# Adding two chunks of squares on VectorE ahead of TensorE's sums over the partitions

## The chip, the cores and the metric

The kernel runs on one core of one Trainium2 chip. The metric is device time in microseconds (us) of one execution. Five engines work side by side, each through its own in-order queue, and wait for one another only by semaphores: TensorE (PE; its weight loads are listed apart, as PEld), VectorE (DVE), ScalarE (ACT), GpSimd (POOL) and SyncE (SP), which issues transfers.

## The reference, cut to what matters

Two layers, each a cross-attention block and a mixture-of-experts block. The change lies in the second layer's cross-attention, a recurrence of three iterations over 4 batches of 512 tokens (`slots`) with 256 features:

```python
def rmsnorm(x, w, eps=EPS):
    return x * jax.lax.rsqrt(jnp.mean(x * x, axis=-1, keepdims=True) + eps) * w
...
for _ in range(NUM_ITERS):                       # 3
    sn = rmsnorm(slots, slot_norm_w)
    q_proj = sn @ Wq.T
    scores = jnp.einsum('bkd,bmd->bkm', q_proj, k_proj) * SCALE
    attn = jax.nn.softmax(scores, axis=-2)
    attn = attn / (jnp.sum(attn, axis=-1, keepdims=True) + EPS)
    updates = jnp.einsum('bkm,bmd->bkd', attn, v_proj)
    slots = gru_cell(updates, slots, gru_wih, gru_whh, gru_bih, gru_bhh)
```

What matters here is `mean(x * x)` over the 256 features of each token.

## The kernel before, in words

The slots of a batch lie turned in SBUF: features on the 128 partitions, in two chunks (`C = 2`), and the 512 tokens along the free dimension, `HT[h]` with the shape 128 x 2 x 512. A batch has 512 tokens in `TT = 4` tiles of `P = 128`. Two batches are worked on in turn, `h` = 0 and 1. There are 12 turns of the recurrence (the text calls them turn 0 to turn 11; `q` in the code): turns 0 to 5 are the three iterations of batches 0 and 1, turns 6 to 11 those of batches 2 and 3. `it` is the iteration: 0 in turns 0, 1, 6 and 7.

The order of the work on each engine is written out by hand in `ORDER_C`, a string of stage names for each engine that `stages_c` reads once per turn `k`. A name with `-` in front belongs to the turn before, a name with `k:` in front is done in turn k alone (`!6,7:` in all but 6 and 7), and the digit at its end is then the batch. What the change touches, with the lines of the kernel:

- ACT `sq` (L1146; in iteration 0 inside `slotT`, L1134) squares `HT[h]` into `squares(h)`, 128 x 2 x 512, a view of the buffer `S1[h]`, and adds 1 to the semaphore `slot_sq`.
- ACT `hi` (L1176; L1132 in iteration 0) rounds the slots to a high part, and DVE `lo` (L1584; L1516 in iteration 0, inside `slotT`) computes the rest, `HTS[h][:, 1]`.
- PE `ss` (L1816 to L1828) waits for `slot_sq` and sums the squares over the partitions: for each of the 4 token tiles and each of the 2 chunks a matmul with the squares as weights and one column of ones as the moving operand, the 2 chunks of a tile accumulated in one column of PSUM. The trace has each of these 8 matmuls in float32 as two instructions, so a turn has 16 (and 16 weight loads).
- DVE `ve` (L1526) waits for these sums, scales them to a mean and adds epsilon. POOL `power` (L941) raises it to -1/2. PE `rsb` (L1834) spreads the four columns of roots over the partitions and turns them into a row with 4 products (8 instructions), ACT `rs` (L1149) moves it out.
- PE `scores` (L1836 to L1847) multiplies the keys with the slots; DVE `mulA`, `mulB` (L1534) scale the scores by that row of roots, and the softmax follows on DVE and ACT (L1538, L1153, L1543, L1138, L1547). PE `upd` (L1857) multiplies with the values, DVE `upd` (L1559) divides, PE `uT` (L1624) turns the result, and the gates of the recurrent cell follow on PE as `ha`, `ra`, `na`, `za`, `hb`, `rb`, `nb`, `zb` (products of three matmuls each, L205 to L207), mixed with the other batch's turn. DVE `ga` (L1568, L1571) and `zb` (L1577, L1579) are parts of the cell on VectorE.

In the order of PE a turn begins with `-ha ... -ra`, then `ss`, then `-na`, then `rsb` and `scores` (in turns 6 and 7 `ss` comes behind `-na`, and `-za` lies between `ss` and `rsb`; in turns 8 and 9 the router's `logits` lie ahead of `ss` and its `lt` ahead of `rsb`). In the order of DVE a turn has `... 6:slotT2 7:slotT3 lo ve ... -ga ...`; in turn 0 `0:slotT0 0:ctxT1` stand ahead of `lo ve`. `ctxT1` is L1511. PE `spin` (L1630) is a run of products of ones that nobody reads.

Around the recurrence: ahead of it the first layer (up to some 470 us of the span), behind it the second layer's routing and experts (from some 900 us).

Of the kernel before, what the change touches and what calls it, by code (L numbers as in the profile page):

```python
# [18 lines left out]
P = 128  # L19
# [10 lines left out]
C = D // P  # L30
# [69 lines left out]
def build(nc, x, ctx_in, cols, rows, wq, wk, wv, wo, pos_bias, w1, w2, router1, m1_w1, m1_w2, ws1, ws2,  # L100
          Wq, Wk, Wv, wih, whh, router2, gate_w, up_w, down_w, down_b, out):
    top = ExitStack()
    with top:
        def sb(name, shape, dt=F32, where=None):
            return (where or top).enter_context(nc.sbuf_tensor(name, shape, dt))
# [3 lines left out]
        def sem(name):  # L109
            if name not in sems:  # L110
                sems[name] = top.enter_context(nc.semaphore(name))
            return sems[name]
# [9 lines left out]
        ones = sb("ones", [P, P])  # L122
# [37 lines left out]
        ve = [sb(f"ve{h}", [P, TT]) for h in two]  # L160
# [22 lines left out]
        def col(name, i=0, n=1):  # L183
            return colv[:, COLS[name][0] + i:COLS[name][0] + i + n]
# [8 lines left out]
        def bank(h, k):  # L193
            return PS[:, 4 * h + k, :]
# [4 lines left out]
        def token_banks(h, k):  # L199

            return banks(h, k).rearrange("p b (a d) -> p (b a) d", d=D)

        def product(pe, out_, a, b, first=True, last=True):

            pe.matmul(out_, a[1], b[0], start=first, stop=False)  # L205
            pe.matmul(out_, a[0], b[1], start=False, stop=False)  # L206
            return pe.matmul(out_, a[0], b[0], start=False, stop=last)  # L207
# [113 lines left out]
        def squares(h):  # L321

            return S1[h][:].rearrange("p (c a) d -> p c (a d)", c=C)

        def updates(n, h):

            return S2[h] if n < 2 else SN[h]

        def gate_slot(h, d, k):

            if d == 0:
                return HB[h][:, 4 + k]
            return (S1[h][:, 0:2].rearrange("p j d -> p (j d)"), S1[h][:, 2:4].rearrange("p j d -> p (j d)"), S0[h][:, 0], S0[h][:, 1])[k]
# [856 lines left out]
        def _(dve):  # L1190
# [169 lines left out]
            for stage, n, h in stages_a("dve"):  # L1360
# [41 lines left out]
                elif stage == "num":  # L1402
# [5 lines left out]
                    for c in range(C):  # L1408
                        ins = dve.scalar_tensor_tensor(out=HB[h][:, 4 + c], in0=S0[h][:, c], scalar=col("bv", c),
                                                       in1=HB[h][:, 6 + c], op0=ALU.add, op1=ALU.mult)  # L1410
# [74 lines left out]
            for stage, n, h, it, q in stages_c("dve"):  # L1485
# [4 lines left out]
                elif stage == "wih":  # L1490
                    after(dve, "wih_hi")
                    for c in range(C):
                        for part, at in zip(wih_sums(c), (slice(0, 2 * D), slice(2 * D, 3 * D))):
                            ins = dve.scalar_tensor_tensor(out=WIH[:, 1, c, at], in0=part, scalar=col("w_in", c), in1=WIH[:, 0, c, at].bitcast(F32),
                                                           op0=ALU.mult, op1=ALU.subtract)
# [12 lines left out]
                elif stage == "ctxT":  # L1508
                    dve.wait_ge(sem("inT_hi"), B + n + 1)
                    for c in range(C):  # L1510
                        ins = dve.scalar_tensor_tensor(out=RT[h][:, 1, c], in0=bank(h, c), scalar=col("w_in", c), in1=RT[h][:, 0, c].bitcast(F32),  # L1511
                                                       op0=ALU.mult, op1=ALU.subtract)
# [4 lines left out]
                elif stage == "kk":  # L1517
                    dve.wait_ge(sem("kk_hi"), key_count(n))
                    for c in range(C):
                        ins = dve.scalar_tensor_tensor(out=KK[h][:, 1, c], in0=bank(h, c), scalar=col("w_slot", c), in1=KK[h][:, 0, c].bitcast(F32),  # L1520
                                                       op0=ALU.mult, op1=ALU.subtract)
                    ins.then_inc(sem("kk_lo"), 1)
                elif stage == "ve":

                    dve.wait_ge(sem("ss_ps"), q + 1)
# [26 lines left out]
                elif stage == "upd":  # L1552
# [5 lines left out]
                    for j in range(TT):  # L1558
                        ins = dve.tensor_scalar(updates(n, h)[:, j], bank(h, j)[:, 0:D], SM[h][:, 4, j:j + 1], None, ALU.mult)  # L1559
# [12 lines left out]
                elif stage in ("za", "zb"):  # L1572
# [6 lines left out]
                    ins = dve.scalar_tensor_tensor(out=HT[h][:, d], in0=gate_slot(h, d, 1), scalar=0.5, in1=gate_slot(h, d, 3), op0=ALU.mult, op1=ALU.add)  # L1579
# [39 lines left out]
        def _(pe):  # L1619
# [13 lines left out]
            def parts(t, *at):  # L1633
                return tuple(t[(slice(None), i) + at] for i in two)
# [26 lines left out]
            for stage, n, h in stages_a("pe"):  # L1661
# [7 lines left out]
                elif stage == "qk":  # L1669
# [6 lines left out]
                    for w in range(2):  # L1676
                        for c in range(C):
                            for c2 in range(C):
                                ins = product(pe, bank(h, 2 * w + c), parts(W3, w, c2, slice(c * P, (c + 1) * P)),
                                              parts(RT[h], c2), c2 == 0, c2 == C - 1)  # L1680
                        ins.then_inc(sem("qk_ps"), 1)
                elif stage == "ewT":
# [3 lines left out]
                    for jc in range(TT):  # L1686
                        for i in range(TT):
                            ins = pe.transpose(bank(0, jc)[:, i * P:(i + 1) * P], band[:, i, jc * P:(jc + 1) * P], ident[:])
                    once(ins, "ewT_ps")
                elif stage == "v":  # L1690
                    pe.wait_ge(sem("th"), n + 1)
                    for j in range(TT):
                        for c in range(C):
                            ins = product(pe, token_banks(h, 0)[:, j], parts(RT[h], c, slice(j * P, (j + 1) * P)),
                                          parts(W3, 2, c), c == 0, c == C - 1)
                    ins.then_inc(sem("v_ps"), 1)
                    pe.wait_ge(sem("ekT"), n + 1)
                    for j in range(TT):
                        for c in range(C):
                            ins = pe.transpose(token_banks(h, 2)[:, j, c * P:(c + 1) * P], S0[h][:, c, j * P:(j + 1) * P], ident[:])  # L1700
                    ins.then_inc(sem("ek_ps"), 1)
                elif stage in ("den", "num"):
# [6 lines left out]
                    for c in range(C):  # L1709
                        for j in range(TT):  # L1710
                            ins = pe.matmul(bank(h, b + c), w[:, j, c * P:(c + 1) * P], EWT[:, j], start=j == 0, stop=j == TT - 1)  # L1711
                    ins.then_inc(sem(f"{stage}_ps"), 1)
                elif stage == "attn":
# [6 lines left out]
                    for j in range(TT):  # L1720
                        for c in range(C):
                            ins = pe.matmul(token_banks(h, 0)[:, j], HB[h][:, 4 + c, j * P:(j + 1) * P], WO[:, c], start=c == 0, stop=c == C - 1)
# [4 lines left out]
                elif stage in ("hidA", "hidB"):  # L1727
                    pe.wait_ge(sem("aT_lo"), C * (n + 1))
                    for m in hidden_of(stage):
                        if m >= 4:  # L1730
                            pe.wait_ge(sem("hidden"), HC * n + m - 3)
                        for c in range(C):
                            ins = product(pe, bank(h, m % 4), parts(W1, c, slice(m * P, (m + 1) * P)), parts(RT[h], c), c == 0, c == C - 1)
                        ins.then_inc(sem("hid_ps"), 1)
                elif stage == "ffn":
                    pe.wait_ge(sem("hidden"), HC * (n + 1))
                    for j in range(TT):
                        for m in range(HC):
                            ins = pe.matmul(token_banks(h, 0)[:, j], HB[h][:, m, j * P:(j + 1) * P], W2[:, m], start=m == 0, stop=m == HC - 1)  # L1739
# [10 lines left out]
                elif stage in ("upA", "upB"):  # L1750
                    for f in (0, 1) if stage == "upA" else (2, 3):
                        if f >= 2:
                            pe.wait_ge(sem("sh_relu"), SC * n + f - 1)
                        for c in range(C):
                            ins = product(pe, bank(h, 2 + f % 2), parts(WS1, c, slice(f * P, (f + 1) * P)), parts(RT[h], c), c == 0, c == C - 1)
# [7 lines left out]
                elif stage == "down":  # L1763
                    pe.wait_ge(sem("sh_sq"), SC * (n + 1))
                    for j in range(TT):
                        for f in range(SC):
                            ins = pe.matmul(token_banks(h, 2)[:, j], HB[h][:, f, j * P:(j + 1) * P], WS2[:, f], start=f == 0, stop=f == SC - 1)
# [11 lines left out]
            for stage, n, h, it, q in stages_c("pe"):  # L1779
                if stage == "gt":  # L1780
                    pe.wait_ge(sem("cw_raw"), 80)
                    for c in range(C):
                        for o in range(C):
                            ins = pe.matmul(PS[:, 7, c * D:(c + 1) * D], raw_k[:, o, c * P:(c + 1) * P], raw_q[:, o], start=o == 0, stop=o == C - 1)
                    once(ins, "gt_ps")
                elif stage == "wih":
                    moe_end(pe, 0, groups, ("y",))
                    for c in range(C):
                        for part, at in zip(wih_sums(c), (slice(0, 2 * D), slice(2 * D, 3 * D))):
                            for k in range(C):  # L1790
                                ins = pe.matmul(part, raw_wv[:, k, c * P:(c + 1) * P], raw_wih[:, k, at], start=k == 0, stop=k == C - 1)
# [17 lines left out]
                elif stage == "kk":  # L1809
                    after(pe, "gt_lo")  # L1810
                    pe.wait_ge(sem("inT_lo"), B + n + 1)
                    for c in range(C):
                        for c2 in range(C):
                            ins = product(pe, bank(h, c), parts(GT, c2, slice(c * P, (c + 1) * P)), parts(RT[h], c2), c2 == 0, c2 == C - 1)
                    ins.then_inc(sem("kk_ps"), 1)
                elif stage == "ss":  # L1816
# [4 lines left out]
                        pe.wait_ge(sem(f"slot_new{h}"), slot_count(n, 0))  # L1821
                    if it == ITERS - 1 and n >= 2:
                        pe.wait_ge(sem("rank_read"), B + n - 1)
                    pe.wait_ge(sem("slot_sq"), q + 1)
                    for j in range(TT):
                        for c in range(C):
                            ins = pe.matmul(bank(h, 2)[:, j:j + 1], squares(h)[:, c, j * P:(j + 1) * P], ones[:, 0:1], start=c == 0, stop=c == C - 1)  # L1827
                    ins.then_inc(sem("ss_ps"), 1)  # L1828
                elif stage == "rsb":
                    if q == 0:  # L1830
# [2 lines left out]
                    for j in range(TT):  # L1833
                        ins = pe.matmul(bank(h, 3)[:, j * P:(j + 1) * P], rstd[h][:, j:j + 1].to_broadcast([P, P]), ident[:], start=True, stop=True)  # L1834
                    ins.then_inc(sem("rsb_ps"), 1)
                elif stage == "scores":  # L1836
# [5 lines left out]
                    for j in range(TT):  # L1842
                        if j == TT - 1:
                            pe.wait_ge(sem("root_rows"), q + 1)
                        for c in range(C):
                            ins = product(pe, bank(h, j), parts(KK[h], c, slice(j * P, (j + 1) * P)), parts(HTS[h], c), c == 0, c == C - 1)
                        ins.then_inc(sem("score_ps"), 1)  # L1847
                elif stage == "upd":
# [5 lines left out]
                    for m in range(TT):  # L1854
                        pe.wait_ge(sem("p_lo"), TT * q + m + 1)
                        for j in range(TT):
                            ins = product(pe, bank(h, j)[:, 0:D + 2], parts(PH[h], m, slice(j * P, (j + 1) * P)), parts(PV[h], m), m == 0, m == TT - 1)  # L1857
# [6 lines left out]
                elif stage in ("ha", "hb", "ra", "rb", "na", "nb", "za", "zb"):  # L1864
# [17 lines left out]
                    for i, (w, o, src, c) in enumerate(factors):  # L1882
                        ins = product(pe, bank(h, b), parts(w, c, slice(o * P, (o + 1) * P)), parts(src, c), i == 0, i == len(factors) - 1)
                    ins.then_inc(sem("gru_ps"), 1)
                elif stage == "final":
# [3 lines left out]
                    for j in range(TT):  # L1889
                        for c in range(C):  # L1890
                            ins = pe.transpose(token_banks(h, 2)[:, j, c * P:(c + 1) * P], HT[h][:, c, j * P:(j + 1) * P], ident[:])
# [69 lines left out]
```

## Time and profile before

| | us |
|---|---|
| three runs before | 1196.59, 1197.67, 1199.54 (median 1197.67) |
| profiled execution | 1196.42 |
| its span, first to last instruction | 1194.6 |
| TensorE busy in it | 1050.8 (88%) |
| VectorE, ScalarE, GpSimd busy | 742.4, 422.6, 351.3 |
| first and last instruction of L1827 (the sums) start at | 475.9 and 863.9 |

All times in rows are counted from the start of the span. A row of the timeline gives start, duration, engine, line, operation, what is written and read, the number of instructions merged, and in brackets how long the engine was idle before, with what released it. Matmul durations overlap: the pace of TensorE is read from starts.

### The profile page before, as it was taken

How to read it: one execution, taken by the hardware profiler on the slowest of the kernel's cores; microseconds unless marked ns; L12 is line 12 of the kernel's file. 1: busy time of each engine (PE TensorE's matmuls, PEld its weight loads, DVE VectorE, ACT ScalarE, POOL GpSimd, SP SyncE). 2: the span in 40 equal slices, each digit the busy share in tenths (PEclk: the TensorE clock that was granted, in tenths of full speed). 3: DMA queues.
4: the chain of work that ended last, by engine and by line, in shares of the span. 5: the costliest groups of instructions: out<-in, count | busy, mean ns of one | idle time of the engine just before them, and what ended most of it. 6: DMA issues, size and time to landing. Idle time of an engine off the chain costs nothing.

```text
span 1194.6 us, 17670 instructions
## 1 busy us (share of the span) xinstructions
PE 1050.8 (88%) x5946; PEld 859.4 (72%) x5946; DVE 742.4 (62%) x1821; ACT 422.6 (35%) x791; POOL 351.3 (29%) x293
## 2 busy tenths in 40 slices
PE   7899989999886886999999999999997399999990
PEld 5557767478465774778888888888885189998990
DVE  5566754774744666666666767556657466666664
ACT  2213132050414653434433445444442243333330
POOL 2505145041233442001111101110242734536510
PEclk9999999999988998899999999999998799999995
DMA  9001025000055565001000000000010685527216
GB/s 334 22 0 36 1 72 160 0 1 1 23 177 177 163 209 188 1 1 36 1 1 1 1 1 1 1 1 1 19 51 32 235 265 157 166 74 241 78 54 229
DMA packets 73267, 95.84 MB, mean 80 GB/s; under 512 B 6128, under 2 KB 59632, under 8 KB 73072
## 3 DMA queue, kind: packets, MB, share of 16 engines
q1 hardware_dynamic: 58576, 65.35, 17.1%
q0 software_dynamic: 14624, 29.64, 7.7%
q8 instruction: 37, 0.61, 0.2%
q14 instruction: 30, 0.25, 0.1%
HBM read 66.23 MB, written 28.74 MB: 79 GB/s over the span
## 4 chain that ended last, share of the span: by engine, by line
PE 48%; DVE 17%; another core or an unknown queue 13%; issue 7%; ACT 5%; DMA 4%; SPq 3%; POOL 3%; DVEq 0%; ACTq 0%; POOLq 0%
PE PS L205 13%; PE PS L207 12%; PE PS L206 12%; PE PS L1739 2%; PE PS L1624 2%; PE PS L1827 2%; PE PS L1711 2%; POOL rstd L941 2%; DMA S<-routed 1%; ACT PH L1138 1%; DVE hs L683 1%; PE PS L1834 1%; DVE act L704 1%; DVE st L1206 1%
## 5 line engine op out<-in xcount | busy, mean ns | idle before, releaser
L941 POOL TENSOR_TENSOR rstd<-ve,minus_half 128x4 f32<-128x4 f32 x40 | 45.3, 1132 | 349.5 <-DVE ve L1213 229.4
L580 POOL DMA_INDIRECT results<-S,place_of x80 | 77.6, 970 | 186.1 <-DVE S L728 102.2
L205 PE MATMUL PS<-xt,split 128*128 128x256 f32 x312 | 89.4, 287 | 10.8 <-issue 7.7
L206 PE MATMUL PS<-xt,split 128*128 128x256 f32 x312 | 88.2, 283 | 0.0
L207 PE MATMUL PS<-xt,split 128*128 128x256 f32 x312 | 88.2, 283 | 0.0
L948 POOL DMA_INDIRECT routed<-S,dest x64 | 65.2, 1019 | 60.7 <-DVE dest L1316 43.4
L653 ACT ACTIVATE act<-PS,colv 128x256 f32<-128x256 f32 x84 | 39.8, 474 | 119.1 <-PE PS L207 91.6
L1630 PE MATMUL PS<-ones_bf 128*128 128x512 bf16 x200 | 57.1, 439 | 19.1 <-DMA routed<-S,dest 13.7
L205 PEld LDWEIGHTS PS<-xt,split 128*128 128x128 f32 x312 | 59.7, 191 | 13.2 <-issue 9.7
L205 PE MATMUL PS<-split,hs 128*128 128x256 f32 x184 | 59.6, 324 | 5.6 <-DVE hs L683 2.9
L704 DVE SCALAR_TENSOR_TENSOR act<-PS,colv,act 128x256 f32<-128x256 f32 x84 | 40.6, 484 | 37.8 <-ACT act L653 31.4
L1711 PE MATMUL PS<-EWT,HB 128*128 128x512 f32 x128 | 57.4, 608 | 3.0 <-DVE EWT L1375 3.0
L207 PEld LDWEIGHTS PS<-xt,split 128*128 128x128 f32 x312 | 59.8, 192 | 0.0
L206 PEld LDWEIGHTS PS<-xt,split 128*128 128x128 f32 x312 | 59.8, 192 | 0.0
L205 PE MATMUL PS<-RT,WIH 128*128 128x512 f32 x144 | 59.0, 410 | 0.0
L205 PE MATMUL PS<-HTS,WHH 128*128 128x512 f32 x144 | 57.4, 398 | 1.0 <-DVE RT L1229 1.0
L207 PE MATMUL PS<-RT,WIH 128*128 128x512 f32 x144 | 57.5, 399 | 0.0
L1022 POOL TENSOR_TENSOR S<-HT,S 128x512 f32<-128x512 f32 x12 | 15.5, 1290 | 142.8 <-ACT S L1169 142.8
L206 PE MATMUL PS<-RT,WIH 128*128 128x512 f32 x144 | 57.3, 398 | 0.0
L207 PE MATMUL PS<-HTS,WHH 128*128 128x512 f32 x144 | 56.5, 393 | 0.0
L1534 DVE TENSOR_TENSOR S<-PS,HB 128x512 f32<-128x512 f32 x48 | 33.1, 689 | 37.8 <-PE PS L207 37.8
L206 PE MATMUL PS<-HTS,WHH 128*128 128x512 f32 x144 | 56.3, 391 | 0.0
(348 smaller groups left out, 3124.2 us busy)
## 6 DMA issues: line engine op xcount, KB each, us to landing
S<-routed SPq DMA_DIRECT2D x44, 264.0 KB, 2.8
HB<-results SPq DMA_DIRECT2D x12, 512.0 KB, 6.6
routed<-blank SPq DMA_DIRECT2D x20, 264.0 KB
raw<-gate_w SPq DMA_DIRECT2D x8, 512.0 KB
raw<-up_w SPq DMA_DIRECT2D x8, 512.0 KB
raw<-down_w SPq DMA_DIRECT2D x8, 512.0 KB
X<-x SPq DMA_DIRECT2D x4, 512.0 KB
raw<-m_w SPq DMA_DIRECT2D x8, 256.0 KB
```

What stands on the lines that cost most here:

```text
L205: pe.matmul(out_, a[1], b[0], start=first, stop=False)
L206: pe.matmul(out_, a[0], b[1], start=False, stop=False)
L207: return pe.matmul(out_, a[0], b[0], start=False, stop=last)
L580: pool.indirect_dma_start(out=results[m], out_offset=bass.IndirectOffsetOnAxis(ap=place_of[:, i, a:a + 1], axis=0), in_=moe[m].y[:, i, a], ...
L653: act.activation(w.act[:, f % 2, 0], PS[:, f, 0:G], ACT.Sigmoid, bias=col("gate_b", b)).then_inc(sem(f"m{m}_act"), 1)
L704: dve.scalar_tensor_tensor(out=a[:, 1], in0=PS[:, f, 0:G], scalar=col("gate_b", e * w.fc + f), in1=a[:, 0], op0=ALU.add, op1=ALU.mult).the ...
L941: pool.tensor_tensor(rstd[h][:], ve[h][:], minus_half[:], ALU.pow).then_inc(sem(name), 1)
L948: pool.indirect_dma_start(out=routed[m], out_offset=bass.IndirectOffsetOnAxis(ap=dest[m][:, n, j, kk:kk + 1], axis=0), in_=S2T[h][:, j], i ...
L1534: step(dve.tensor_tensor(scaled(h, j), bank(h, j), root_rows(h), ALU.mult))
L1624: ins = pe.transpose(bank(h, k + c)[:, j * P:(j + 1) * P], src[:, j, c * P:(c + 1) * P], ident[:])
L1630: pe.matmul(free.rearrange("p (a b) -> p a b", b=P), ones_bf[:], ones_bf[:].unsqueeze(1).to_broadcast([P, TT, P]), start=True, stop=True)
L1711: ins = pe.matmul(bank(h, b + c), w[:, j, c * P:(c + 1) * P], EWT[:, j], start=j == 0, stop=j == TT - 1)
```

## The change

VectorE gets a new stage `sqs` ahead of `lo` in every turn. It waits until ScalarE's squares are there, adds the second chunk's squares to the first chunk's in place (128 x 512, float32), and counts `slot_sq` up again, so that the semaphore rises by 2 in a turn. TensorE waits for the second count and sums one chunk only: 4 matmuls, 8 instructions, in a turn.

```diff
     "dve": ("ctxT0 gt0 pv0 kk0 combine0 slotsA0 slotsB0 wih0",
...
-            "6:slotT2 7:slotT3 lo ve 0:combine1 -ga ...
+            "6:slotT2 7:slotT3 sqs lo ve 0:combine1 -ga ...
...
+                elif stage == "sqs":
+                    dve.wait_ge(sem("slot_sq"), 2 * q + 1)
+                    dve.tensor_tensor(squares(h)[:, 0], squares(h)[:, 0], squares(h)[:, 1], ALU.add).then_inc(sem("slot_sq"), 1)
                 elif stage == "ve":
...
-                    pe.wait_ge(sem("slot_sq"), q + 1)
+                    pe.wait_ge(sem("slot_sq"), 2 * q + 2)
                     for j in range(TT):
-                        for c in range(C):
-                            ins = pe.matmul(bank(h, 2)[:, j:j + 1], squares(h)[:, c, j * P:(j + 1) * P], ones[:, 0:1], start=c == 0, stop=c == C - 1)
+                        ins = pe.matmul(bank(h, 2)[:, j:j + 1], squares(h)[:, 0, j * P:(j + 1) * P], ones[:, 0:1], start=True, stop=True)
                     ins.then_inc(sem("ss_ps"), 1)
```

## Rows read from the trace of the kernel before

**Rows 1.** The page: busy time with share and instructions; the chain's shares.

```profile
PE 1050.8 (88%) x5946; PEld 859.4 (72%) x5946; DVE 742.4 (62%) x1821; ACT 422.6 (35%) x791; POOL 351.3 (29%) x293
PE 48%; DVE 17%; another core or an unknown queue 13%; issue 7%; ACT 5%; DMA 4%; SPq 3%; POOL 3%; DVEq 0%; ACTq 0%; POOLq 0%
```

**Rows 2.** Windows: stretch, length, busy of each engine, PEclk, DMA share, GB/s.

```profile
509.00:900.00 391.00, 380.06 (x2096) 322.18 (x2097) 249.06 (x564) 167.80 (x283) 67.17 (x56) 0.99 0.03 9
```

**Rows 3.** Timeline of turn 3, around the sums.

```profile
580.77 1.06 ACT L1146 ACTIVATE S<-HT 128x1024 f32<-128x1024 f32 x1 [0.18 <-DVE HT L1579]
...
582.45 1.84 PE L1827 MATMUL PS<-ones,S 128*128 128x1 f32 x16
...
582.81 1.23 DVE L1584 TENSOR_TENSOR HTS<-HT,HTS 128x1024 fp32r<-128x1024 f32 x1 [2.08 <-ACT HTS L1176]
...
584.15 0.48 PE L205 MATMUL PS<-RT,WIH 128*128 128x512 f32 x1
...
584.33 0.16 DVE L1526 TENSOR_SCALAR ve<-PS 128x4 f32<-128x4 f32 x1 [0.29 <-PE PS L1827]
...
584.57 1.38 POOL L941 TENSOR_TENSOR rstd<-ve,minus_half 128x4 f32<-128x4 f32 x1 [5.93 <-DVE ve L1526]
...
586.00 1.16 PE L1834 MATMUL PS<-ident,rstd 128*128 128x128 f32 x8 [0.23 <-POOL rstd L941]
```

**Rows 4.** Chain that ended last: start, length, engine and line, ahead of turns 3, 8.

```profile
571.51 1.67 DVE S L1559 x4
573.23 1.10 PE PS L1624 x8
...
764.98 0.34 PE PS L205
```

**Rows 5.** Timeline of turn 1, around the sums.

```profile
513.21 1.84 PE L1827 MATMUL PS<-ones,S 128*128 128x1 f32 x16
...
514.92 0.48 PE L205 MATMUL PS<-RT,WIH 128*128 128x512 f32 x1
...
515.09 0.16 DVE L1526 TENSOR_SCALAR ve<-PS 128x4 f32<-128x4 f32 x1 [6.35 <-PE PS L1827]
```

**Rows 6.** Timeline of turn 8, around the sums.

```profile
763.13 1.84 PE L1827 MATMUL PS<-ones,S 128*128 128x1 f32 x16
...
765.25 1.39 POOL L941 TENSOR_TENSOR rstd<-ve,minus_half 128x4 f32<-128x4 f32 x1 [8.16 <-DVE ve L1526]
...
766.73 1.16 PE L1834 MATMUL PS<-ident,rstd 128*128 128x128 f32 x8
```

**Rows 7.** Timeline of turn 6, around the sums.

```profile
687.82 1.21 DVE L1516 TENSOR_TENSOR HTS<-HT,HTS 128x1024 fp32r<-128x1024 f32 x1
...
689.09 1.95 PE L1827 MATMUL PS<-ones,S 128*128 128x1 f32 x16 [0.17 <-DVE HTS L1516]
...
690.89 0.48 PE L205 MATMUL PS<-HTS,WHH 128*128 128x512 f32 x1
```

**Rows 8.** Timeline of turn 0, around the sums.

```profile
475.74 1.40 DVE L1511 SCALAR_TENSOR_TENSOR RT<-PS,colv,RT 128x512 fp32r<-128x512 f32 x2
...
475.92 3.54 PE L1827 MATMUL PS<-ones,S 128*128 128x1 f32 x16 [3.33 <-DVE HTS L1516]
...
479.33 2.72 PE L1630 MATMUL PS<-ones_bf 128*128 128x512 bf16 x6
```

**Rows 9.** One line's instructions: min/median/max ns, first and last start.

```profile
L1427 DVE TENSOR_TENSOR RT<-S,RT x8: 693/1764/2859, 80.6 to 254.9; 128x512 fp32r<-128x512 f32 x8
```

**Rows 10.** Timeline at 457 us: GpSimd and VectorE side by side.

```profile
456.77 3.44 POOL L1018 TENSOR_TENSOR WHH<-HB,WHH 128x1536 fp32r<-128x1536 f32 x1
...
457.34 3.95 DVE L1551 TENSOR_TENSOR PV<-EMB,PV 128x1024 fp32r<-128x1024 f32 x1 [6.06 <-ACT PV L1143]
```

**Rows 11.** Windows: from the sums to `rsb` in turns 6 and 7.

```profile
689.00:695.10 6.10, 6.01 (x29) 5.15 (x30) 2.61 (x5) 0.46 (x1) 1.38 (x1) 0.76 0.00 0
729.70:734.40 4.70, 4.63 (x28) 4.15 (x29) 2.59 (x5) 0.44 (x1) 1.38 (x1) 1.00 0.00 0
```

2 rows, old and new, of the table ORDER_C are left out of this document.

## The prediction

> **What bounds the kernel now.** I read the page first, then the windows of the stage, then the chain, then the timeline around each of the twelve groups of sums. On the page the reader sees TensorE busy for 88% of the span and with the largest share of the chain, and VectorE next [rows 1]. In the recurrence this is tighter: between 509 and 900 us TensorE is busy 380.06 of 391 us, VectorE 249.06, at a granted clock of 0.99 [rows 2]. So time taken off TensorE there can move the end, unless a partner chain takes over at once. The chain says where it does: into turn 3 it enters TensorE from VectorE's L1559 and stays on TensorE up to the sums [rows 4]. From the sums it leaves to VectorE's L1526 and GpSimd's power and comes back at `rsb`, for which TensorE waits 0.23 us [rows 3]. In turn 8 it goes straight on over TensorE's next product [rows 4], and `rsb` has no wait [rows 6]. The ends that matter are thus the start of `rsb` in each turn: behind it stand scores, softmax, update and gates, all of which begin from it, and behind turn 11 the routing and the experts, serial as well. I carry a shift of `rsb` to the end one to one.
>
> **The change part by part.** *The sums.* Sixteen instructions take from 513.21 to 514.92, the start of the next product: 1.71 us when TensorE comes to them without a pause [rows 5], and 1.80 (689.09 to 690.89) behind a pause [rows 7]. Eight take half: 0.85, or 0.90 behind a pause. At half clock, in turn 0, sixteen take 3.41 (475.92 to 479.33), eight 1.71 [rows 8].
>
> *The pair-add.* The trace has this form once as a line: two inputs from SBUF, 128x512, L1427, 693 ns at the least and 2859 at the most [rows 9]. I take 0.69, because what makes it long is seen elsewhere: L1551, 3.95 us long, starts at 457.34 while GpSimd's L1018 runs from 456.77 to 460.21 [rows 10], and it ends 1.08 us after that. In turn 3 GpSimd has been idle for 5.93 us when the power starts at 584.57 [rows 3], in turn 8 for 8.16 [rows 6]: nothing of GpSimd's lies beside the add. The upper end, 2.86, stays for the range.
>
> The Trainium skill has the rule that speaks against the change (SBUF — State Buffer, "Who interferes with whom"): a VectorE instruction with two SBUF inputs contends with a GpSimd one that reads SBUF, and the later one stands still. The two rows at 457 us agree. By that rule too the add costs its bare length here, since the neighbour is missing; the sum is the same, but an add moved beside GpSimd's L1022 would pay.
>
> *Turns 2, 3, 4, 5, 10, 11* (the rows are turn 3's; the other five repeat it within 0.05 us). ScalarE's squares end at 581.83. The add starts 0.03 us later, as L1584 does behind ScalarE, and ends at 582.55, in VectorE's 2.08 us of idle ahead of L1584 at 582.81 [rows 3]: the cover is 0.26 us, and `lo` does not move. TensorE would start its sums at 582.45 and now waits until 582.60 (0.05 us from VectorE's end to TensorE's start, as from 689.03 to 689.09 [rows 7]). The next product starts at 583.50 in place of 584.15. The sums are there at 583.68 (L1526 comes 0.18 us behind that start now), but VectorE is in `lo` until 584.04 [rows 3]. So L1526 starts between 583.96 (VectorE's neighbours overlap by up to 0.08) and 584.04, not 584.33: 0.29 to 0.37 earlier, I take 0.33. `lo` is what is late next. Six turns: 1.98 us. Queued behind the adding instruction on VectorE are `lo`, L1526 and `ga`. If the add were 0.3 us longer they would begin to slip.
>
> *Turns 8 and 9.* The squares and `lo` are done before TensorE comes (it has the logits first); the add is hidden. The sums, as long as in turn 1 (1.84 us busy in both [rows 5, 6]), save 0.85. GpSimd's power, now ended at 766.64, 0.09 ahead of `rsb` [rows 6], moves by the same 0.85, so nothing stands in the way: 1.70 for both.
>
> *Turn 1.* VectorE has been idle for 6.35 us when the sums end at L1526, far more than the add takes: it is hidden, and the sums save 0.85 [rows 5].
>
> *Turns 6 and 7.* Here the add stands behind L1516 in VectorE's queue, which ends at 689.03 and is what TensorE waits for now [rows 7]. The add ends at 689.64, the sums start at 689.69 instead of 689.09, and take 0.90 instead of 1.80: 0.30 is left. `rsb` follows on TensorE's own work. Both: 0.60.
>
> *Turn 0.* The order puts L1511 between L1516 and the add. It ends at 477.14, the add at 477.75, TensorE starts at 477.80 instead of 475.92 [rows 8]: 1.88 late, and at half clock saves 1.71: a loss of 0.17, say 0.2. It ends in spins and `rsb` on TensorE, so it counts.
>
> *Sum.* 1.98 + 1.70 + 0.85 + 0.60 - 0.2 = 4.93 us. Against the profiled execution: its span 1194.6 becomes 1189.7, its time 1196.42 becomes 1191.5. The median shown, 1197.67, lies 1.25 above that execution; on its scale the forecast is 1192.7. No transfer is issued by a moved step, and SP's and POOL's orders are untouched.
>
> *The clock.* In turn 6 the granted clock is 0.76 between the sums and `rsb`, and this stretch takes 6.10 us; in turn 7, with the same work behind the same wait, it is 1.00 and 4.70 [rows 11]. The same prelude gives a fall or none, and a fall costs about 1.3 us (from the sums to `rsb`, 5.97 against 4.65). The change alters the prelude in both directions: a pause longer by 0.60 and a one-column stretch shorter by 0.90. I count nothing, and keep -1.3 (the fall of turn 6 gone) and +1.3 (one more). In turn 0 TensorE is silent for 1.9 us more while at 1.2 GHz; if its clock comes back as much later, twice the work of 1.9 us at 2.4 GHz stretches by 0.95. I keep that for the range.
>
> The skill's rule (TensorE: Matmul & The Clock Gate, "What's actually happening") is that the clock follows TensorE's recent activity and is half by default. By it longer pauses bring falls, which is rival C below; turn 6 agrees with it, turn 7, with the same pause and no fall, does not decide it [rows 11]. The sum stays.
>
> **The rivals.**
> *A: the small gain.* The hand-over costs more than I took: the add ends 0.3 us later in the six turns (longer dispatch, or a slower write in place), so the 0.33 goes to nearly 0; and turn 0 loses 0.95 more by the clock. 4.93 - 1.98 - 0.95 = 2.0: 1195.7. For it: the cover is 0.26 us only. Against it: VectorE's lengths repeat within a few ns.
> *B: the full gain.* All twelve turns save the whole 0.85, as an instruction count has it (11 x 0.85 + 1.71 = 11.1): 1186.6. Against it stands `lo` ahead of L1526 in six turns. The way to it would be VectorE taking L1526 first, which an in-order queue cannot.
> *C, on the other side: the clock falls at the new pause.* Eight turns (2 to 7, 10, 11) get a pause ahead of the sums or a longer one. If each brought turn 6's fall, that is 7 new falls of 1.3, 9.1 us against 4.9 gained: 1201.9. It decides from the seventh fall (3.6 us over the old time need 8.5 us); three falls make it no change. For it: turn 6 falls after such a wait. Against: turn 7 does not, and in six of the turns the pause is only 0.15 us by matmul starts, and half of the one-column work behind it is gone.
> *D: the add is slowed by GpSimd*, as L1427's worst case, 2.86 us, everywhere: the add ends 2.17 later. Six turns lose about 1.5 each (`lo` then ends at 585.9 and L1526 starts at 585.85), turns 6 and 7 1.9 each, turn 0 2.4; turn 1 gains 0.85 and turns 8 and 9 some 0.2 each: 1197.7 + 9.0 + 3.8 + 2.4 - 1.25 = 1211.6. No row puts GpSimd beside it; it has hardly a chance.
>
> **How the numbers follow.** Chances: forecast 0.62, A 0.25, B 0.04, C 0.06, D 0.01, and 0.02 for something I don't see. About 0.3% (3.6 us) is what a measurement of this kernel can tell from no change. The forecast lies 4.9 below, 1.3 from that bound, and one clock fall or 1 us of median would carry it over: of its 0.62 I give 0.54 to faster and 0.08 to no change. A is no change but for 0.03; B is faster. C gives 0.04 to slower and 0.02 to no change, D 0.01 to slower, the rest 0.01 each way. Faster 0.61, within 0.3% 0.33, slower 0.06. The forecast's own range is 1190.3 to 1195.5: 1.3 each way for a fall and about 1.1 for the runs' spread (1196.59 to 1199.54). The range reaches down to 1189.5, and up over A to 1197.5.
>
> **What would show it.** L1827 with 96 instructions; a VectorE add of 0.69 us in every turn, in turn 3 ended 0.2 to 0.3 us ahead of L1584; TensorE waiting 0.1 to 0.4 us for it in eight turns; L1526 directly behind L1584, idle before it 0 and not 0.29; `rsb` 0.3 us earlier relative to L1584 in six turns; in turn 0 a TensorE wait of about 5.2 us where 3.33 stood. The spans from turn to turn, `rsb` to `rsb`, shorter by these terms. It is wrong if the add is longer than 0.9 us, if the granted clock falls in turns where it did not, or if a turn's gain is missing one turn later, which would mean another chain than that of `rsb`.

## The result

| | before | after |
|---|---|---|
| median of the runs, us | 1197.84 | 1189.07 |
| range, us | 1196.59 to 1199.54 | 1188.08 to 1191.14 |
| profiled execution and its span, us | 1196.42, 1194.6 | 1190.02, 1188.3 |

The ratio after to before is 0.9929, 95% interval 0.9917 to 0.9940: 8.5 us faster, where 4.9 were forecast, and 0.4 us below the low end of the range. Two more groups of runs gave 0.9923 (0.9911 to 0.9936) and 0.9939 (0.9918 to 0.9960). The direction was right and the size wrong.

TensorE is 12.9 us less busy on the page, VectorE 8.1 more, as twelve adds of 0.69 make it:

```profile
PE 1037.9 (87%) x5850; PEld 845.0 (71%) x5850; DVE 750.5 (63%) x1833; ACT 423.4 (36%) x791; POOL 350.8 (30%) x293
```

Turn 3 after, to be laid beside [rows 3]. In the changed kernel L1525 is the add, L1829 the sums, L1529 what was L1526, L1587 what was L1584 (`lo`), L1836 `rsb`. Columns as in the rows of before:

```profile
580.47 0.69 DVE L1525 TENSOR_TENSOR S<-S 128x512 f32<-128x512 f32 x1 [1.13 <-ACT S L1146]
...
581.22 1.05 PE L1829 MATMUL PS<-ones,S 128*128 128x1 f32 x8
...
581.42 1.23 DVE L1587 TENSOR_TENSOR HTS<-HT,HTS 128x1024 fp32r<-128x1024 f32 x1 [0.26 <-ACT HTS L1176]
...
582.13 0.48 PE L205 MATMUL PS<-RT,WIH 128*128 128x512 f32 x1
...
582.56 0.15 DVE L1529 TENSOR_SCALAR ve<-PS 128x4 f32<-128x4 f32 x1
...
582.80 1.39 POOL L941 TENSOR_TENSOR rstd<-ve,minus_half 128x4 f32<-128x4 f32 x1 [5.55 <-DVE ve L1529]
...
584.24 1.16 PE L1836 MATMUL PS<-ident,rstd 128*128 128x128 f32 x8 [0.48 <-POOL rstd L941]
```

The reader is to see the hidden add (it runs in time that VectorE had idle, and VectorE is still idle for 0.26 us ahead of `lo`), the next product 0.91 us behind the start of the sums instead of 1.70, and L1529 without idle time behind `lo`. From `lo` to `rsb` it is 2.82 us now (581.42 to 584.24) and was 3.19.

Turn 6 after, to be laid beside [rows 7] and [rows 11]: the add and the sums, and the window from the sums to `rsb`.

```profile
686.42 0.69 DVE L1525 TENSOR_TENSOR S<-S 128x512 f32<-128x512 f32 x1
...
687.26 1.02 PE L1829 MATMUL PS<-ones,S 128*128 128x1 f32 x8 [0.87 <-DVE S L1525]
```

```profile
687.20:691.10 3.90, 3.84 (x21) 3.34 (x22) 2.58 (x4) 0.00 (x0) 1.38 (x1) 1.00 0.02 4
```

The window of turn 7, 726.10 to 730.00, is as long and at a granted clock of 1.00 too. Before, one of the two turns was at 0.76 and 6.10 us. TensorE is now idle for 0.87 us ahead of the sums, 0.70 more than the 0.17 of [rows 7]: 0.61 for the add, and a hand-over of 0.15 us (687.11 to 687.26) where 0.06 stood (689.03 to 689.09).

**The table on which the rest goes.** From each profile I took the start of `rsb` in every turn. T0 is the time from VectorE's L1516 of turn 0 to the `rsb` of turn 0, the others are the time from one `rsb` to the next. The stage is their sum; the head is what lies ahead of that L1516, the tail from the last `rsb` to the end of the span.

```
us              head    T0   T1+T2   T3    T4    T5   T6+T7   T8    T9   T10   T11   stage   tail
before         474.59  7.25  71.34 32.82 32.81 32.91  82.70 32.31 34.18 32.91 32.05  391.28 328.73
b_again        473.79  7.25  72.14 32.83 32.81 32.90  82.71 32.33 34.20 32.88 32.05  392.10 328.71
b_third        475.12  7.24  72.06 32.82 32.84 32.85  82.69 32.30 34.16 32.94 32.03  391.93 329.65
b_fourth       473.70  7.25  72.30 32.86 32.84 32.91  82.55 32.49 34.17 32.90 32.02  392.29 329.71
after          473.77  7.50  70.53 32.44 32.43 32.51  80.76 31.44 33.29 32.51 31.65  385.06 329.47
a_again        475.67  7.50  69.45 32.46 32.42 32.48  80.74 31.44 33.26 32.50 31.66  383.91 328.52
a_third        475.88  7.50  70.15 32.45 32.43 32.51  80.69 31.39 33.29 32.56 31.67  384.64 329.38
e1_sums_only   471.51  5.54  70.05 32.47 32.42 32.48  79.34 31.40 33.28 32.52 31.65  381.15 329.84
e2_add_only    474.97  9.21  72.30 34.36 34.23 34.29  84.79 32.32 34.18 34.01 32.85  402.54 330.19
e6_no_lo_wait  471.49  7.25  72.40 32.83 32.84 32.87  80.27 32.31 34.18 32.93 32.01  389.89 327.62
e3_ve_first    475.66  7.50  69.62 32.76 32.72 32.78  80.68 31.91 33.75 32.84 32.01  386.57 327.57
e4_turn0       472.40  6.19  70.67 32.44 32.42 32.52  80.69 31.45 33.28 32.52 31.67  383.85 327.95
e7_all_moved   474.87  6.18  71.14 32.73 32.69 32.78  78.73 31.91 33.75 32.86 32.00  384.77 327.66
e8_best        476.03  6.18  69.94 32.49 32.42 32.53  78.73 31.45 33.28 32.54 31.67  381.23 329.14
```

The turns repeat to some hundredths, the head moves by up to 5 us and the tail by 2 from one execution to the next. A term of the sum is read from the turns, not from the time of a run.

### The profile page after: what moved, and what is told of

Its sections match the earlier page's. It is cut to its first block, busy times and chain, and to the rows that moved or that the text cites. A ratio compares the mean times of both kernels' runs of the same rounds, so it can differ in the third digit from the quotient of the medians.

```text
span 1188.3 us, 17490 instructions
## 1 busy us (share of the span) xinstructions
PE 1037.9 (87%) x5850; PEld 845.0 (71%) x5850; DVE 750.5 (63%) x1833; ACT 423.4 (36%) x791; POOL 350.8 (30%) x293
## 4 chain that ended last, share of the span: by engine, by line
PE 46%; issue 19%; DVE 18%; ACT 7%; DMA 4%; POOL 3%; SPq 2%; DVEq 0%; ACTq 0%; POOLq 0%
PE PS L205 13%; PE PS L207 11%; PE PS L206 11%; PE PS L1742 2%; DMA S<-routed 2%; PE PS L1714 2%; PE PS L1627 2%; POOL rstd L941 2%; ACT PH L1138 1%; DVE hs L683 1%; PE PS L1836 1%; DVE st L1206 1%; DVE act L704 1%; PE PS L1633 1%; DVE HT L1582 1%
```

## The experiments

The runs fall into three groups, each on a chip of its own with its own runs of the kernel before (medians 1197.62, 1193.42, 1197.69). Times are compared within a group.

**b_again, b_third, b_fourth: the kernel before, unchanged.**

> The kernel before, once more, for its own spread and for the fall of the clock in turn 6. Theory (terms plus clock): of the 8.8 us between the medians, 4.9 are the terms of the sum and 1.3 the fall in turn 6; if that fall belongs to the kernel before and not to one execution, turn 6 is again at a granted clock of about 0.76 between the sums and rsb, 5.97 us from the start of the sums to rsb. Rival (chance): it is 1.00 and 4.65 us, and the fall comes in some executions only. Time ratio to the kernel before 1.000 +- 0.001 by both.

> The kernel before, a third profile: theory (its wait and its sixteen instructions bring a fall): one fall in turns 6 or 7, so that the two together take 82.7 us as in both profiles so far, against 81.4 without; ratio 1.000. Rival: none, 81.4.

> The kernel before, a fourth profile: as for the third; by the theory again a fall in turn 6 or 7.

The ratios were 0.9994 (0.9979 to 1.0008) and 0.9995 (0.9981 to 1.0009); b_fourth was one execution, 1197.50 us. All three profiles have one fall of the clock in turn 6 or 7, like the first. In b_again it is turn 7's, not turn 6's as the theory had it:

```profile
689.00:693.80 4.80, 4.71 (x29) 4.20 (x30) 2.62 (x5) 0.47 (x1) 1.38 (x1) 1.00 0.00 0
728.10:734.50 6.40, 6.31 (x29) 5.35 (x30) 2.62 (x5) 0.47 (x1) 1.38 (x1) 0.73 0.00 0
```

In b_third and b_fourth it is turn 7's as well. The fall costs about 1.6 us (6.40 against 4.80 for the same work). Turn 6 and turn 7 together take 82.55 to 82.71 us in all four: which turn is hit changes, that one is hit did not. What decides between the two no run shows. The rival, that it is chance whether there is one at all, has four profiles against it.

**a_again, a_third: the changed kernel, unchanged.**

> The changed kernel, once more, in five rounds. Theory: the ratio comes out between 0.9929 and 0.9959 (8.5 to 4.9 us); in turns 2 to 5, 10 and 11 rsb is again 0.37 to 0.40 us earlier per turn, in turn 6 there is no fall. Rival (something beyond the terms saves time in every execution): ratio again 0.9929 and no fall in either kernel's turn 6, so that 3 us are to be found elsewhere.

> The changed kernel, a third time, to weigh the turns and the spread. Theory: turn by turn as in its two profiles (32.4 to 32.5 us for turns 3 to 5, 41.8 and 38.9 for turns 6 and 7), ratio 0.9923 to 0.9945. Rival (falls of the clock merely happened to be absent): a fall in turn 6 or 7, 43.1 or 40.2.

Medians 1189.09 and 1191.20 us, ratios 0.9923 (0.9911 to 0.9936) and 0.9939 (0.9918 to 0.9960). No fall in turn 6 or 7 in any of the three profiles: 80.69 to 80.76 us together. The difference to before is 1.93 us. Turn 6 alone, where it had no fall, took 42.00 to 42.04 us before (b_again, b_third, b_fourth) and takes 41.81 to 41.83 after: 0.2. The step from the sums to the next product is 0.92 shorter (1.81 to 0.89), the pause ahead of it 0.70 longer. So of the 1.93 us some 0.4 are shorter sums in the two turns, and 1.5 are a fall that is gone.

**e1_sums_only: the saving without the add.** The second chunk's squares are left out of the sum.

```diff
-            "6:slotT2 7:slotT3 sqs lo ve ...
+            "6:slotT2 7:slotT3 lo ve ...
-                    pe.wait_ge(sem("slot_sq"), 2 * q + 2)
+                    pe.wait_ge(sem("slot_sq"), q + 1)
-                    dve.tensor_scalar(ve[h][:], bank(h, 2)[:, 0:TT], 1.0 / D, 1e-6, ...
+                    dve.tensor_scalar(ve[h][:], bank(h, 2)[:, 0:TT], 2.0 / D, 1e-6, ...
```

> The changed kernel without the add and the wait for it: TensorE sums the first chunk alone (8 instructions), the mean is scaled by 2/D; the second chunk's squares are left out, so the routing behind may differ and the turns are what counts. Theory (lo holds L1526 back): turns 2 to 5, 10 and 11 gain no more than with the add, 0.37 to 0.40 each; turns 6 and 7 gain 0.90, turn 0 1.7, turns 1, 8, 9 0.85: from turn 0 to the rsb of turn 11 about 3 us shorter than the changed kernel (8.2 to 8.4 us against the kernel before, clock falls aside), some 1186. Rival (the pause for the add is what limits the six turns): they too gain 0.85 each, 11 us in all, some 1183.

Median 1185.01 us, ratio 0.9899 (0.9885 to 0.9913), stage 381.15, 3.4 us shorter than the changed kernel's mean of 384.54. Turns 3, 4, 5, 10 and 11 are as long as with the add, to 0.02 us. The timeline of turn 3 shows why; TensorE starts its sums without a pause and ends them at 577.2, and L1529 still starts when `lo` lets go:

```profile
576.40 0.95 PE L1829 MATMUL PS<-ones,S 128*128 128x1 f32 x8
576.76 1.23 DVE L1587 TENSOR_TENSOR HTS<-HT,HTS 128x1024 fp32r<-128x1024 f32 x1 [2.07 <-ACT HTS L1176]
577.21 0.48 PE L205 MATMUL PS<-RT,WIH 128*128 128x512 f32 x1
577.90 0.15 DVE L1529 TENSOR_SCALAR ve<-PS 128x4 f32<-128x4 f32 x1
```

So in these turns the add and its pause cost nothing, and `lo` caps the gain. The add costs 1.96 us in turn 0 (7.50 against 5.54) and 1.4 in turns 6 and 7 together.

This run also halves the sums of turns 6 and 7 and leaves the pause of the kernel before ahead of them (0.18 us idle). Neither turn has a fall; turn 6:

```profile
681.80:685.70 3.90, 3.87 (x21) 3.36 (x22) 2.58 (x4) 0.41 (x1) 1.39 (x1) 1.00 0.02 4
```

**e2_add_only: the add and the wait without the saving.**

```diff
-                    dve.tensor_tensor(squares(h)[:, 0], squares(h)[:, 0], squares(h)[:, 1], ALU.add).then_inc(sem("slot_sq"), 1)
+                    dve.tensor_tensor(spare[:], squares(h)[:, 0], squares(h)[:, 1], ALU.add).then_inc(sem("slot_sq"), 1)
                     pe.wait_ge(sem("slot_sq"), 2 * q + 2)
                     for j in range(TT):
-                        ins = pe.matmul(bank(h, 2)[:, j:j + 1], squares(h)[:, 0, j * P:(j + 1) * P], ones[:, 0:1], start=True, stop=True)
+                        for c in range(C):
+                            ins = pe.matmul(bank(h, 2)[:, j:j + 1], squares(h)[:, c, j * P:(j + 1) * P], ones[:, 0:1], start=c == 0, stop=c == C - 1)
```

> The changed kernel with the add written to a spare tile and TensorE still summing both chunks (16 instructions), waiting for the add: its cost alone. Theory: turns 2 to 5, 10, 11 lose 0.15 to 0.25 each against the kernel before (TensorE starts its sums 0.15 later and takes 0.09 longer), turns 6 and 7 0.6 each, turn 0 1.9, the others nothing: 4 to 4.5 us, 1202. Rival (the pause brings falls of the clock): in addition 1.3 us for each turn at 0.76 instead of 1.00, up to 1211. Rival (the pause costs nothing because something else is later): 1198.

Median 1205.97 us, ratio 1.0065 (1.0052 to 1.0078), 7.8 us slower than before by the ratio: the rival with the clock is right. The terms are there (turn 0 1.96 us longer, as worked out), and beyond them the clock falls in turns 2, 3, 4, 5, 7, 10 and 11, seven of them. The profiled execution is the slowest of the five (1204.04 to 1209.48 us) and has the lowest mean granted clock of them, 0.946 against 0.950 to 0.954, so the others may have fewer. Turn 3:

```profile
586.21 0.69 DVE L1526 TENSOR_TENSOR spare<-S 128x512 f32<-128x512 f32 x1 [1.13 <-ACT S L1147]
...
586.96 1.95 PE L1831 MATMUL PS<-ones,S 128*128 128x1 f32 x16
...
589.56 0.63 PE L206 MATMUL PS<-RT,WIH 128*128 128x512 f32 x1
```

The same products that take 0.39 us each at full clock take 0.63 from 589.56 on. The window over it has a granted clock of 0.83:

```profile
586.90:590.90 4.00, 4.00 (x24) 3.40 (x24) 1.99 (x3) 0.79 (x2) 1.39 (x1) 0.83 0.02 4
```

The pause that in the changed kernel lies ahead of eight instructions and brings no fall brings one in seven of eight turns ahead of sixteen. The eighth is turn 6: TensorE is idle for 0.87 us ahead of its sixteen, and there is no fall, for which no run shows the reason:

```profile
698.10:702.90 4.80, 4.72 (x29) 4.24 (x30) 2.58 (x4) 0.00 (x0) 1.38 (x1) 1.00 0.00 0
```

**e6_no_lo_wait: the kernel before, without the wait of turns 6 and 7.** Nothing of the change is in it.

```diff
                     if it == 0:
-                        pe.wait_ge(sem(f"slot_lo{h}"), split_count(n, 0))
+                        if n < 2:
+                            pe.wait_ge(sem(f"slot_lo{h}"), split_count(n, 0))
                         pe.wait_ge(sem(f"slot_new{h}"), slot_count(n, 0))
```

> The kernel before with one edit: in turns 6 and 7 the sums no longer wait for VectorE's L1516, only for the squares; nothing of the change is in it. In both profiles of the kernel before one of turns 6 and 7 had a fall of the clock behind the sums (1.3 us), in both of the changed kernel none. Theory (the fall comes of the wait plus the long one-column stretch): without the wait no fall in either turn, and 0.4 to 0.6 us saved on the wait in each: about 2.2 us in all against the kernel before, 1195.4. Rival (the fall is bound to the time in the run or to the 16 instructions, not to the wait): one fall stays, 1.0 us saved, 1196.6.

The two turns take 80.27 instead of 82.66 us, and neither has a fall, although the sixteen instructions are all there. Turn 6 (turn 7, 725.10 to 730.00, is at 1.00 too):

```profile
686.40:691.30 4.90, 4.90 (x31) 4.29 (x31) 3.17 (x5) 1.02 (x2) 1.38 (x1) 1.00 0.00 0
```

Median 1189.76 us, ratio 0.9969 (0.9947 to 0.9990), 3.7 us with an interval from 1.2 to 6.3; the turns give 2.4 (0.9 of shorter waits, 1.5 of the fall), the rest is head and tail. It is one profile, on a chip on which the kernel before was not profiled; that the interval lies above 0.9 us speaks for a fall in the kernel before there too. With e1 and e2 this has both halves: sixteen one-column instructions without the pause bring no fall, a pause ahead of eight brings none, and a pause ahead of sixteen brings one in seven of the eight turns of e2 and in one of the two of the kernel before.

**e3_ve_first: L1529 ahead of `lo`.**

```diff
-            "6:slotT2 7:slotT3 sqs lo ve ...
+            "6:slotT2 7:slotT3 sqs ve lo ...
```

> The changed kernel with L1529 (before: L1526) ahead of lo on VectorE. Theory (lo holds it back in six turns): in turns 2 to 5, 10, 11 it starts about 0.24 us earlier and rsb with it; 1.4 us faster than the changed kernel, some 1187.6. Rival (lo, now later by 0.9 us, is needed by the scores or delays ga): equal or slower, 1189 to 1191.

A miss. L1529 does start earlier, 1.09 us behind the start of the sums instead of 1.34. But `rsb` comes 2.22 us behind L1529 instead of 1.68, and turns 3 to 5 are 0.3 us longer than in the changed kernel, turns 8 and 9 by 0.47. Turn 3:

```profile
583.32 0.16 DVE L1529 TENSOR_SCALAR ve<-PS 128x4 f32<-128x4 f32 x1 [1.15 <-PE PS L1829]
583.40 1.22 DVE L1587 TENSOR_TENSOR HTS<-HT,HTS 128x1024 fp32r<-128x1024 f32 x1
583.57 1.92 POOL L941 TENSOR_TENSOR rstd<-ve,minus_half 128x4 f32<-128x4 f32 x1 [5.32 <-DVE ve L1529]
...
585.54 0.97 PEld L1836 LDWEIGHTS PS<-ident,rstd 128*128 128x128 f32 x8 [1.20 <-POOL rstd L941]
```

GpSimd's power takes 1.92 us beside `lo`, which has two inputs in SBUF. What it takes alone, and what it took in the kernel before, the trace of before shows; L1568 has two inputs in SBUF as well, and the power of turn 3 starts at 584.57 and takes 1.38 [rows 3]:

```profile
569.00 1.01 POOL L941 TENSOR_TENSOR rstd<-ve,minus_half 128x4 f32<-128x4 f32 x1 [12.04 <-DVE ve L1352]
...
584.40 0.68 DVE L1568 SCALAR_TENSOR_TENSOR HB<-HB 128x512 f32<-128x512 f32 x1
```

So the power takes 1.01 us alone, 1.38 beside the short L1568, and 1.92 beside the long `lo`. The rule of the Trainium skill weighed in the prediction (SBUF — State Buffer, "Who interferes with whom") names this pair, and the rows agree with it: had the power stood still from its start until `lo` ended at 584.62 and then taken its 1.01 us, it would have ended at 585.63; it ended at 585.49, as if 0.14 us of its work had gone ahead. Beside L1568, which ends at 585.08, the same reckoning gives 586.09, and it ended at 585.95. So in the kernel before and in the changed one, too, a neighbour lengthens the power by 0.37 us or a little more in turns 1 to 11; no run moves it away.

The median was 1191.01 against 1193.42, ratio 0.9985 (0.9964 to 1.0007). The changed kernel was not run on this chip; by the turns 3 to 5 and 8 to 11, e3 gives back 2.5 of the 7.4 us that the change gives.

**e4_turn0: the add of turn 0 ahead of L1511.**

```diff
-            "=zb 0:slotT0 0:ctxT1 ...
+            "=zb 0:slotT0 0:sqs0 0:ctxT1 ...
-            "6:slotT2 7:slotT3 sqs lo ve ...
+            "6:slotT2 7:slotT3 !0:sqs lo ve ...
```

> The changed kernel with the add of turn 0 ahead of L1511 on VectorE. Theory (turn 0 lost 0.2 because the add stood behind L1511): the sums of turn 0 start 0.7 us behind L1516's end instead of 2.0, and from L1516 of turn 0 to the rsb of turn 0 1.3 us are saved. Rival (the turn-0 loss is bound to the clock): TensorE's rise to full clock comes no earlier and less than half of it is left at the scores.

T0 is 6.19 instead of 7.50 us: the 1.3 us that were expected. One execution, 1185.90 us.

**e7_all_moved and e8_best.** e7 has e4's move, e3's, and in turns 6 and 7 the add ahead of L1516 with e6's edit; e8 is e7 with `lo` again ahead of L1529.

```diff
-            "6:slotT2 7:slotT3 sqs lo ve ...
+            "6:sqs2 7:sqs3 6:slotT2 7:slotT3 !0,6,7:sqs ve lo ...    # e7
+            "6:sqs2 7:sqs3 6:slotT2 7:slotT3 !0,6,7:sqs lo ve ...    # e8
```

> The changed kernel with all three: L1529 ahead of lo, the add of turn 0 ahead of L1511, and in turns 6 and 7 the add ahead of L1516 and the sums no longer waiting for L1516. Theory: 1.4 + 1.3 + 2 x 0.9 = 4.5 us faster than the changed kernel, some 1184.6. Rival (VectorE's later lo takes over in turns 6 and 7, or the clock takes the rest): 2 to 3 us.

> The changed kernel with the two moves that held: the add of turn 0 ahead of L1511, and in turns 6 and 7 the add ahead of L1516 with sums that wait only for the squares; lo stays ahead of L1529. Theory (terms add up turn by turn): turn 0 6.19 us from L1516 to rsb, turns 6 and 7 1.0 us shorter each, turns 2 to 5, 8 to 11 as in the changed kernel: 3.3 us faster than the changed kernel, a ratio to the kernel before near 0.990. Rival (what is saved is given back by the clock or by a later stage): 1 us or less under the changed kernel.

e7: 1186.93 us, ratio 0.9943 (0.9925 to 0.9961); turns 6 and 7 are 2.0 us shorter than in the changed kernel, T0 is 1.3 shorter, e3's part takes 2.5 of these 3.3 us back, and turns 1 and 2 are 1.1 longer, which is within what they vary by (stage 384.77). e8: 1188.39 us, ratio 0.9921 (0.9900 to 0.9943), beside 0.9939 for the changed kernel on the same chip (1191.20). Its stage is 381.23, 3.3 us under the changed kernel's mean, as the terms add up to; in the times of runs the 2.8 us between the medians are within the spread of both. It is the shortest stage of a kernel that computes everything.

## Why the prediction was wrong

By its own steps, means of four profiles before and three after.

| step | forecast | turns | |
|---|---|---|---|
| turns 3, 4, 5, 10, 11 | 5 x 0.33 = 1.65 | 1.94 | right; 0.39 each, just above 0.29 to 0.37 |
| turns 8, 9 | 1.70 | 1.83 | right |
| turn 0 | -0.2 | -0.25 | right |
| turns 1, 2 | 0.85 + 0.33 | 1.92 | 0.74 more; falls in turn 2 that vary |
| turns 6, 7, sums | 0.60 | 0.4 | 0.2 too much: the hand-over to TensorE takes 0.15 us, not 0.05 |
| turns 6, 7, clock | 0 | 1.5 | **the step that failed** |
| sum | 4.93 | 7.37 | |

*The clock.* "I count nothing, and keep -1.3 (the fall of turn 6 gone) and +1.3 (one more)" is the step that failed. I read two turns, one with a fall and one without, as chance, with equal weight to both sides. The kernel before has one fall in this pair in four profiles of four, the changed kernel none in three. The rows had a hint that I noted and did not weigh: the pause was to grow by 0.60 (it grew by 0.70), but the one-column stretch behind it was to shrink by 0.90 (0.92). The fall was priced at 1.3 because its part behind `rsb` was left out; it costs 1.5 to 1.6. e1, e6 and e2 show that the two act together: take away either, the pause or half of the instructions, and no fall is left in turns 6 and 7. This is shown by how often falls come; which of two like turns is hit stays open.

*Rival C* had the mechanism and the wrong sign for this change. Falls at the pause in seven turns came true in e2, but only where sixteen instructions stay. Their price there is lower than mine: the stage is 10.6 us longer than before, 5.1 of it the terms by the starts in its trace (1.96 + 4 x 0.27 + 2 x 0.33 + 2 x 0.70), and with the one fall of the kernel before set against them seven falls come to some 7.1 us, 1.0 each. I priced the pause as if halving the instructions had no part in the clock.

*Turns 1 and 2* gained 1.92 and not 1.18 (before 71.34 to 72.30 us, after 69.45 to 70.53). Turn 1 alone gained 0.75, near its 0.85, with 1 us between profiles of one kernel. Turn 2 gained 1.17 where 0.33 was forecast, and the granted clock says where the rest is. From 536 to 544 us it is 0.79 in three profiles of before and in two of after; their turn 2 takes 36.41 to 36.60 and 36.20 to 36.24 us, a gain of 0.32. In b_fourth it is 0.57, and turn 2 takes 37.83; in a_again it is 1.00, and turn 2 takes 34.62. So the surplus is a fall of the clock that was longer in one profile of before and absent in one of after; that the change has a part in this is not shown.

*What limits the six turns* was right: `lo` holds L1526 back (e1), the add is hidden with 0.26 us to spare, and it lasts 0.68 to 0.69 us. Rival B (a full gain everywhere) is out by e1, rival A (the cover fails) by the timeline, rival D (the add slowed by GpSimd) by the 0.69 us; e3 shows the contention the other way round, with GpSimd as the one that waits.

*The rest.* The turns give 7.4 us, the spans of the profiles 6.6 (means 1195.4 and 1188.8), the runs 7.3 to 9.2 us. The head differs by up to 5 us between executions of one kernel, with nothing of the change in it, so one microsecond between the turns and the runs stays open. The range did add 1.3 us for a fall and 1.1 for the runs below the forecast (1192.7 to 1190.3; above it the same sum gives 1195.1, not the 1195.5 written there), and went down to 1189.5. It failed by 0.4 us because the fall that was gone cost 1.5, turn 2 gave 0.8 more by the clock, and the microsecond between turns and runs came on top of both. That turns 6 and 7 gave 0.2 too little and the seven turns 3 to 5 and 8 to 11 0.4 more than forecast moves it less.

## What to carry to other kernels

A saving on a busy engine is worth what stands at the place where its result is taken up: halving the sums gave 0.9 us where TensorE went on from them, and 0.39 where VectorE was busy with something else until later. Where a profile shows a fall of TensorE's clock behind a pause and a run of one-column products, take a few more profiles of the same kernel before calling it chance; shortening either part can take the fall away, and a new wait ahead of such a run can bring one in nearly every turn. Before an instruction with two inputs in SBUF is put behind one that starts GpSimd, look at what GpSimd will then be doing. Even in the kept order such a neighbour lengthens the power by 0.37 us in turns 1 to 11.

## What was not expected of the hardware

- One fall of the clock costs 1.0 us (mean of seven in e2) to 1.6 us (turn 7 of b_again) here and needs little: 16 one-column instructions (1.8 us) without a pause bring none (turns 2 to 5 before, e6), a pause with 8 of them (turns 6, 7 after: 0.87 us idle, 1.02 us of sums) none, the same 16 with 0.15 us more between the last product's start and the first sum bring one in turns 2 to 5 of e2. Turn 6 of e2, with 0.87 us idle ahead of its 16, has none.
- GpSimd's power on 128x4 values takes 1.01 us alone, 1.38 when it starts 0.17 us into VectorE's 0.68 us instruction with two inputs in SBUF, and 1.92 when it starts 0.17 us into one of 1.22 us: it ends 0.87 us behind VectorE's end in both cases.
- Executions of the kernel before on the second chip lay between 1188.84 and 1198.18 us with a median of 1193.42, against 1197.6 on the others: a comparison across chips would have been off by as much as half of the effect.
